# Cross attention's keys in tiles of 128 and 26 instead of 77 and 77, with a new order of all engines

## The reference

```python
def attention(x, ctx, Wq, Wkv, Wo, bo):
    q = x @ Wq
    k, v = jnp.split(ctx @ Wkv, 2, axis=-1)
    out = lowmem_attention(heads_to_batch(q), heads_to_batch(k), heads_to_batch(v))
    return batch_to_heads(out) @ Wo + bo
...
x = attention(ln32(x, ln1_s, ln1_b), ln32(x, ln1_s, ln1_b), Wq1, Wkv1, Wo1, bo1) + x
x = attention(ln32(x, ln2_s, ln2_b), context, Wq2, Wkv2, Wo2, bo2) + x
x = geglu_ff(ln32(x, ln3_s, ln3_b), Wff1, bff1, Wff2, bff2) + x
...
attn = jax.nn.softmax(jnp.einsum('bqf,bkf->bqk', qp, kp), axis=-1)
return jnp.einsum('bqk,bkf->bqf', attn, vp) + q
```

## Time and profile before

| | us |
|---|---|
| median of 3 runs | 1638.75 |
| lowest, highest | 1636.75, 1639.05 |
| span of the profiled execution | 1641.9 |

### The profile page before, as it was taken

The page is one execution under the profiler, slowest core; times in us unless marked ns, Lnnn a source line. Parts: engine busy times, 40 slices in busy tenths (PEclk is TensorE's granted clock), DMA queues, the critical chain, the costliest instruction groups (busy, mean ns, idle before and its releaser), DMA issues.

```text
span 1641.9 us, 33969 instructions
## 1 busy us (share of the span) xinstructions
PE 1557.9 (95%) x12833; PEld 1011.8 (62%) x12833; DVE 1103.1 (67%) x2269; ACT 995.2 (61%) x2024; POOL 252.9 (15%) x342
## 2 busy tenths in 40 slices
PE   6899999999999999999999999999999999998887
PEld 5454545675757666675767667565656656574766
DVE  4667776858676776858677686858677675843433
ACT  4365667666667566666657566666656555664342
POOL 1210412111112021111112021010011010101110
PEclk9999999999999999999999999999999989997999
DMA  9914242555231412645131321356121311303210
GB/s 236 206 39 139 69 71 83 103 108 109 63 84 46 82 51 72 113 98 119 58 86 47 70 58 58 80 98 116 44 73 35 71 42 44 82 31 73 56 34 13
DMA packets 177116, 129.76 MB, mean 79 GB/s; under 512 B 40975, under 2 KB 168889, under 8 KB 176697
## 3 DMA queue, kind: packets, MB, share of 16 engines
q1 hardware_dynamic: 176889, 127.58, 33.0%
q10 hardware_dynamic: 64, 0.02, 0.0%
HBM read 79.24 MB, written 47.71 MB: 77 GB/s over the span
## 4 chain that ended last, share of the span: by engine, by line
PE 71%; DVE 14%; DMA 7%; ACT 3%; SPq 2%; issue 2%; POOL 0%; DVEq 0%; ACTq 0%; POOLq 0%
PE ps_o L1709 11%; PE ps_max L1679 10%; PE ps_last L1622 10%; PE ps_s L1697 9%; PE ps_last L1631 6%; DVE mxh L1360 6%; PE ps_pre L1486 4%; PE ps_cross L1590 4%; DVE mx L1286 3%; PE ps_pre L1494 3%; PE ps_cross L1576 3%; DMA o_s<-den_c 2%; DMA den<-o_s 2%; PE ps_last L1644 1%; PE ps_last L1659 1%
## 5 line engine op out<-in xcount | busy, mean ns | idle before, releaser
L1360 DVE TENSOR_REDUCE mxh<-ps_max 128x1 f32<-128x512 f32 x1024 | 655.8, 683 | 175.2 <-PE ps_max L1679 173.3
L1143 ACT ACTIVATE probs<-ps_s 128x512 f32<-128x512 f32 x1024 | 579.4, 597 | 232.2 <-PE ps_s L1697 185.4
L1679 PE MATMUL ps_max<-kst,qst 96*128 96x512 bf16 x1024 | 371.5, 386 | 22.0 <-DVE mxh L1360 14.7
L1697 PE MATMUL ps_s<-qst,kst 98*128 98x256 bf16 x2048 | 368.2, 275 | 6.1 <-ACT probs L1143 4.3
L1697 PEld LDWEIGHTS ps_s<-qst,kst 98*128 98x128 bf16 x2048 | 178.8, 98 | 146.6 <-ACT probs L1143 49.4
L1709 PE MATMUL ps_o<-probs,vg 128*17 128x256 f32 x4096 | 268.4, 384 | 0.0
L1679 PEld LDWEIGHTS ps_max<-kst,qst 96*128 96x128 bf16 x1024 | 96.0, 97 | 146.5 <-DVE mxh L1360 91.2
L1087 ACT ACTIVATE probs<-ps_cross 77x512 f32<-77x512 f32 x224 | 132.7, 592 | 78.1 <-PE ps_cross L1576 77.2
L1318 DVE SCALAR_TENSOR_TENSOR th<-th,gb 128x256 f32<-128x256 f32 x128 | 56.9, 445 | 164.3 <-ACT gb L1118 164.3
L1709 PEld LDWEIGHTS ps_o<-probs,vg 128*17 128x17 f32 x4096 | 96.5, 97 | 110.4 <-issue 49.8
L1622 PE MATMUL ps_last<-y_hi,wff_hi 128*128 128x256 f32 x448 | 139.6, 312 | 4.8 <-DVE y_lo L1312 2.5
(11 more groups left out here) (261 smaller groups left out, 1951.7 us busy)
## 6 DMA issues: line engine op xcount, KB each, us to landing
parts_s<-qk_parts SPq DMA_DIRECT2D x28, 384.0 KB, 4.3
o_s<-o_sb SPq DMA_DIRECT2D x64, 128.0 KB, 2.6
o_s<-o_sb SPq DMA_DIRECT2D x32, 256.0 KB, 2.2
oT<-o_s SPq DMA_DIRECT2D x62, 128.0 KB
den<-o_s SPq DMA_DIRECT2D x62, 128.0 KB
q_s<-qk_parts SPq DMA_DIRECT2D x16, 384.0 KB, 2.3
q2st<-q_s SPq DMA_DIRECT2D x16, 384.0 KB, 5.3
q2st<-q_s SPq DMA_DIRECT2D x48, 128.0 KB, 6.1
```

The lines of the kernel that those rows point to most:

```text
L1143: nc.scalar.activation(probs[:, step % PR, 2 * pair:2 * pair + 2, :].rearrange("p j q -> p (j q)"), ps_s[pair][:, :], ACT.Exp, scale=SCALE ...
L1360: nc.vector.tensor_reduce(mxh[:, i % PAIRS, i // PAIRS:i // PAIRS + 1], ps_max[i % 2][:, :], AX_X, ALU.max).then_inc(g_mx, 1)
L1679: mm(ps_max[i % 2][:, :], qst[0:ROWS, h, q * P:(q + 1) * P], kst[0:ROWS, h, half * 512:(half + 1) * 512], start=True, stop=True).then_inc( ...
L1697: last = mm(ps_s[pair][:, j * CH:(j + 1) * CH], kst[:, h, kt * P:(kt + 1) * P], qst[:, h, :], start=True, stop=True)
```

## The change

The 154 keys of a head are split 128 + 26 (padded to 32) instead of 77 + 77. A tile `S` holds the first 128 keys of two heads: two matmuls with 128 columns. A tile `A` holds the last 26 keys of eight heads: eight matmuls with 32 columns, four heads side by side in column tiles of 32, twice. So a chunk has 8 `S` and 2 `A` tiles and 10 exps of 128x512 instead of 32 matmuls and 16 exps of 77x512. The values of four heads are one full f32 matmul with `v2b` (block diagonal: 4 x 32 rows against 4 x 32 columns, the rest zero) and four with 17 columns with `v2a`, accumulated in the same place. `CROSS_STEPS` goes from 36 to 30. Five memsets are new on GpSimd (zeros for the padding and `v2b`), the batch's values are loaded by five DMAs instead of one, and a few waits are added (on the memsets; on `g_o`, self attention's last copy, before the last stage's second set of buffers is loaded in the last iteration). The tables of letters are new, one for each iteration.

```diff
-PR2 = 5
+PR2 = 3
+NA = P
+NB = 32
+CTXP = NA + NB
+ORDER2 = ("A0", "S0", "S1", "S2", "V0", "S3", "V1", "A1", "S4", "S5", "S6", "V2", "S7", "V3")
...
-PRE_STEPS, MID_STEPS, CROSS_STEPS, LAST_STEPS = 8, 9, 36, 26
+PRE_STEPS, MID_STEPS, CROSS_STEPS, LAST_STEPS = 8, 9, 30, 26
...
-STEADY = (
-    "uoMSMlcSmpMSMMSSMMSlMMSMcSSMMcVlMMSScclcMuMSScVQSSlccTSSlVScSMcS"
+ORDERS = (
+    "sssppsssspMMspsMMsMpMMssMsMMMMMMMMQpTsMMsMMpp",
...
-                sp.dma_start(v2[:, :, :], v2_s.rearrange("(b a p) n -> b p a n", b=B, p=CT)[b]).then_inc(c_v2, 16)
+                sp.wait_ge(s_const, 13)
+                rows = v2_s.rearrange("(b n) m -> b n m", b=B)[b]
+                sp.dma_start(v2a[:, :], rows[0:NA, :]).then_inc(c_v2, 16)
+                for j in range(G):
+                    sp.dma_start(v2b[j * NB:j * NB + CTX - NA, :, j * W:j * W + VW],
+                                 rows[NA:CTX, :].rearrange("n (g j w) -> j n g w", g=HG, j=G)[j]).then_inc(c_v2, 16)
...
                 if o != NCH - 2:
                     sp.wait_ge(c_s3, min(o, NCH - 2))
+                else:
+                    sp.wait_ge(g_o, NU)
...
+            for i in range(3):
+                nc.gpsimd.memset(k2_part[i][:, :, :, CTX:CTXP], 0.0).then_inc(s_const, 1)
+            pool.wait_ge(s_const, 11)
+            nc.gpsimd.memset(k2st[ROWS:ROWS + SHIFT, :, CTX:CTXP], 0.0).then_inc(s_const, 1)
+            pool.wait_ge(s_const, 12)
+            nc.gpsimd.memset(v2b[:, :, :], 0.0).then_inc(s_const, 1)
...
+                            act.wait_ge(c_s, o * NE2 + x + 1)
+                            if name[0] == "A":
+                                act.wait_ge(c_av, o * 4 + 2 * i)
+                                tile = p2b
+                            else:
+                                act.wait_ge(c_av, o * 4 + (max(0, i - PR2) // 2 + 1 if i >= PR2 else 0))
+                                tile = p2a[:, i % PR2, :]
+                            nc.scalar.activation(tile, cross_banks[spare][x % 2][:, :], ACT.Exp,
+                                                 scale=SCALE).then_inc(c_e, 1)
...
-                        for a in range(2):
-                            last = mm(cross_banks[spare][h % 2][0:CT, a * CH:(a + 1) * CH], k2st[:, at, a * CT:(a + 1) * CT],
-                                      q2st[:, at, :], start=True, stop=True)
...
+                            mm(ps_cross[:, 0:CH], v2b[:, i, :], p2b[:, i % 2 * CH:(i % 2 + 1) * CH], start=True, stop=False)
+                            for j in range(G):
+                                h = G * i + j
+                                last = mm(ps_cross[j * W:j * W + VW, 0:CH], v2a[:, h * VW:(h + 1) * VW],
+                                          p2a[:, h // 2 % PR2, h % 2 * CH:(h % 2 + 1) * CH], start=False, stop=True,
+                                          tile_position=(0, j * W))
...
+                        if name[0] == "A":
+                            for u in range(2):
+                                for j in range(G):
+                                    last = mm(bank[j * NB:(j + 1) * NB, u * CH:(u + 1) * CH],
+                                              k2st[:, stack_at((2 * i + u) * G + j), NA:CTXP],
+                                              q2st[:, stack_at((2 * i + u) * G + j), :], start=True, stop=True,
+                                              tile_position=(0, j * NB))
+                        else:
+                            for u in range(2):
+                                last = mm(bank[:, u * CH:(u + 1) * CH], k2st[:, stack_at(2 * i + u), 0:NA],
+                                          q2st[:, stack_at(2 * i + u), :], start=True, stop=True)
```

More of the change, by code:

```diff
@@ L740, in cross @@
                                  part[:, :]).then_inc(c_shl, 16)
[L741 removed]
+                for _ in range(9):
                     yield
                 store_o2(o, 0)
[L744 removed]
+                for _ in range(6):
                     yield
```

203 lines of the change are left out of this document (109 added, 94 removed).

## The result

The changed kernel takes 1621.59 us (median of four runs, 1615.31 to 1623.90). The kernel before took 1637.98 us beside it. The ratio is 0.9882, with a 95% interval of 0.9858 to 0.9906: faster by 1.2%. The forecast was 1602 and the range 1584 to 1627, so the time lies in the range, but the gain is 16 us by the medians and 19 by the ratio, where 37 were forecast. The profiled execution spans 1618.1 us (1641.9 before), so the traces differ by 23.8 us.

The account below looks back on a forecast made before the run. TensorE's slots were taken as the bound, with some 5 to 9 us of waits per iteration. Terms -20.7, -0.7, -3.5, -8, -7.2 and +3.0 sum to -37.1: profiled 1641.9 to 1604.8, so forecast 1602 against the runs' median, range 1584 to 1627.

Parts of the forecast that it names:

- Cross scores: Cross-stage score matmuls on TensorE: 55.3 us before, -20.7 with A tiles four abreast; bounds 9.7 and nothing saved.
- cross values: Cross-stage value matmuls on TensorE: one full matmul and one tiled set replace two sets, nothing saved.
- A tiles do not overlap: Rival on the cross scores: the 20.7 us are gone and the rest stays, so 1622 us; chance 11%.
- Runs of tiled work: Entering and leaving column tiles on TensorE, 0.22 us a run: 273 runs instead of 276, -0.7 us.
- The last iteration: Six fewer exps in the last chunk, where ScalarE and TensorE alternate: -3.5 us, bounds 0 and 7.1.
- The new order: New tables: -8 us from less waiting at maxima, -7.2 from a lost stall and half clock at chunk 12.
- DMA: More DMA issues on SyncE for a batch's values delay 1/den at chunks 4 and 8: +3.0 us, 0 to 6.
- GpSimd: Five more memsets at the start, 2 us, covered by idle time before the second chunk's rstd: 0.
- ScalarE: Fewer exps take 57 us off ScalarE's busy time; nothing booked for it in the steady state.
- only the work goes: Rival: stalls come back elsewhere as VectorE and ScalarE are nearly as full; -18.4, so 1620 us; chance 20%.
- The slower rival: VectorE waits in order on a DMA, TensorE idles, half clock follows: 7.2 us a time, slower from six places; chance 8%.
- The sign that I named as refuting: New dips in the granted-clock row in mid-program would show the forecast wrong; no 10 us of half clock was expected there.

Follow-up runs that it names:

- e1_tiles: The new tiles of 128 and 26 keys in the old order tables of the kernel before; 1638.17 us, 0.9983 of the kernel before.
- e6_xearly: The changed kernel with the cross stage's loads issued 8 to 20 steps earlier, ahead of den's load; 1638.23 us, 0.9971 of the kernel before.
- e3_v2late: The changed kernel with the five loads of a batch's values issued nine steps into the cross stage; 1618.76 us, 0.9855 of the kernel before.

## Why the prediction was right or wrong

Against the span: forecast -37.1, measured -23.8.

*Cross scores* (-20.7) and *cross values* (0): right in sum. Over the whole program the cross stage's matmuls on ps_cross and ps_s fell from 158.5 to 137.9 us from start to start, by 20.6. The scores alone fell by 23.1 (some 1.8 of it because less of them ran at half clock), and the values rose by 2.8. An A tile between two value groups takes two slots (815.64 to 815.86):

```profile
814.77 1.05 PE L1762 MATMUL ps_o<-probs,vg 128*17 128x256 f32 x16
815.64 0.40 PE L1637 MATMUL ps_cross<-q2st,k2st 98*32 98x256 bf16 x8
815.86 1.05 PE L1762 MATMUL ps_o<-probs,vg 128*17 128x256 f32 x16
```

Its eight matmuls start 5 to 8 ns apart within each four. The bounds of 9.7 and 0, and the rival "A tiles do not overlap", are out.

*Runs of tiled work* (-0.7): right, as far as it goes: 273. e1_tiles shows what the neighbours in the order were worth: 322 runs and no gain.

*The last iteration* (-3.5): too small. From the fourteenth transposed maxima on the program takes 21.5 us less, of which the scores' share is 4. The half clock there fell from 33.4 to 10.9 us, which gives back up to 11 us, and idle times fell by 5.7. I had looked at ScalarE's waits and not at the clock behind them.

*The new order* (-8 and -7.2). The maxima's idle time fell from 22.0 to 17.9, not by half. But maxima and scores outside half clock take 10.3 us less in all (238 to 235 ns a record, and 129 to 125). I hadn't booked that. TensorE changes between the two kinds less often, with 319 pairs of maxima in a row instead of 168 (counted at full clock and where no idle time stands between). A step from a score to a maximum takes 0.15 to 0.16 us where one from score to score takes 0.12, and one from maximum to score took 0.23 in the kernel before where one from maximum to maximum took 0.25. From these four I estimate 1.5 us for the fewer changes; the rest is open, and no run tests it. At chunk 12 nothing went: in place of 2.12 us and 10.2 at half clock TensorE idles 3.13 us at 1321.4, now for the norm, with 6.8 at half clock.

Here I had also misread whose load it was. The load of den_c at 1307.16 is the last stage's. The mid stage's follows its load of x, in the kernel before at 1345.34:

```profile
1344.71 0.52 SPq L691 DMA_DIRECT2D x<-in_x_dram  x1
1345.34 0.56 SPq L672 DMA_DIRECT2D den_c<-o_s  x1
```

The third pair of the order rows sets the last stage's load of before beside the mid stage's of after. In the changed kernel the last stage's load stands ahead of the batch's loads, and behind them stands its store of 1/den, followed by the reload that TensorE waits for:

```profile
1300.46 0.60 SPq L681 DMA_DIRECT2D den_c<-o_s  x1
...
1306.12 3.41 SPq L745 DMA_DIRECT2D v2b<-v_s  x4
...
1311.57 0.59 SPq L685 DMA_DIRECT2D o_s<-den_c  x1
```

```profile
1321.40 3.78 PE L1528 MATMUL ps_last<-wo,oT 128*128 128x256 f32 x8 [3.13 <-DVE oT L1283]
```

So the new order moved the batch's loads from one step of the same path to the next.

*DMA* (+3.0, bounds 0 and 6): **this step failed.** It measured +20.6, as counted above, and 5.5 us more of TensorE's waits for loads of keys, queries and stacks. Three things were wrong in it. I took the issue of a DMA as 0.38 us from the row of v2; the four narrow ones take 3.41 (0.85 each) at chunk 8 and 0.80 in the median. I charged chunks 4 and 8 only, where the earlier trace rows and one row like it showed a wait; in the changed kernel VectorE waits on this path at most chunks, also where no batch starts. And I read its row as a place with a wait, not as a path that had no slack: in the kernel before, 14 to 18 us lie between den's load and the norm in the first nine chunks, and at four of them VectorE already waited, 0.2 to 1.7 us. The new tables have 36 to 61 places from d to the third l step, 44 to 64 in the old ones, and e or f up to 60 behind i. The distance from d alone doesn't decide it: in the new tables the chunk with 61 places waits 2.8 us, and in the old ones a chunk with 44 waits 0.3. What stands between, in SyncE's queue and in flight, decides with it.

*GpSimd* (0): right. The five memsets end at 5.23 us, and GpSimd is still idle 2.67 before the second chunk's variance.

*ScalarE*: 52.7 us less busy, 57 forecast: 605 ns for an exponential of the cross stage where 590 was taken, and 599 instead of 597 in self attention.

*The rivals.* The time is that of "only the work goes" (1620), but not by its reason: VectorE's pace did not put the stalls back, a path of DMAs did for the most part. The slower rival had the mechanism right (VectorE's in-order wait on a DMA, then half clock), and its price per place, 7.2 us, was too high: nine waits of 0.3 to 5.1 us with slow matmuls behind them cost 20.6 more than the eight waits of the kernel before. I gave it its place at den's load, and in the changed kernel it sits at the norm; e6_xearly shows it where I had put it. The sign that I named as refuting, new dips of the clock in mid-program, is what came.

## What to carry to other kernels

When an order is laid out anew, price the DMA round trips that it carries before the slots that it saves: list for each the distance from issue to use and what else is issued in between, before and after, and take one without slack as a cost even if today's trace shows almost no wait there. Follow one load by its stage and not by its name alone, when two stages have one of the same name. A wait of a few microseconds on TensorE is often paid a second time by the clock. And where such a path was late here, neither more distance behind it nor another queue helped, as the next user or the DMA engines were as full; what helped was to ask for the reload as soon as its input is there and to take the batch's values out of its window, in tables that also have the spacing.

## What the runs showed of the hardware

The issue time of a DMA on SyncE depends on its shape. A narrow load of 26 rows in four groups of 17 columns took 0.80 us in the median of 16, the full-width load of the same tensor beside it 0.38 (both above). Shape isn't all: in e3_v2late the same full-width load took 1.05 us once. The landing time depends on what is in flight, whichever engine issued it: the store of 1/den (16 x 8 x 32) took 1.8 us alone and up to 8.6 behind the cross loads, den's load 2.0 and 7.2.

Column-tiled bf16 matmuls of 98 rows start mostly 3 to 8 ns apart in one slot. Each has a weight load of 97 ns of its own, and beside attention values the tile still takes no more than its two slots (0.22 us).

In the middle of the changed kernel half clock came with all five waits of TensorE over 2 us (2.36 to 5.13), with three of the five waits of 1.77 to 1.85 us, and with none of the shorter ones, for 3.4 or 6.8 us each time.
